# Routing one sequence earlier, folds of the queries in row groups, first rows tile by tile, and the last sequence's end by halves, in a two-layer recurrent/attention kernel

## The reference, cut to what matters

```python
x = L0_attn_h                                  # (8, 512, 256)
xn = _layernorm(x)
s = two gated recurrences over the tokens      # "minGRU", W0 then W1, each 256 -> 768
g = silu(top-1 routed expert MLP of xn)        # 8 experts, 256 -> 1024 -> 256, token by token
x = x + s * g
xn = _layernorm(x)
s = RWKV-like recurrence of xn                 # 16 heads, state 16x16 per head,
                                               # o = silu(g) * _ln(ys); s = o @ oW.T
g = silu(latent attention of xn, then a top-2 routed MLP of 8 experts and a shared one)
return x + s * g
```

## Time and profile before

| | |
|---|---|
| median of 3 runs | 2155.03 us (2154.07 to 2158.08) |
| the profiled execution: its own time | 2154.19 us |
| its span in the profile | 2152.3 us, 37412 instructions |
| busy: PE, DVE, ACT, POOL | 94%, 82%, 45%, 39% |
| phase A, B, C begin at | 0, 241.2, 541.2 us |

### The profile page before, as it was taken

One profiled execution on the slowest core, in us unless ns is written; L12 is line 12 of the kernel. 1 busy time (PEld: TensorE's weight loads), 2 busy tenths in 40 slices (PEclk: granted clock), 3 DMA queues, 4 the chain that ended last, 5 costly groups with the idle time before them and its releaser, 6 DMA issues.

```text
span 2152.3 us, 37412 instructions
## 1 busy us (share of the span) xinstructions
PE 2021.3 (94%) x11786; PEld 1235.5 (57%) x11787; DVE 1754.9 (82%) x2890; ACT 979.1 (45%) x2532; POOL 835.9 (39%) x666
## 2 busy tenths in 40 slices
PE   7998599999799999999999999999999999999996
PEld 4554399999446545644564465456445645654563
DVE  5998466665389888889888989898898888899886
ACT  3544244443248236623833472275238235722841
POOL 1335300000353345347434633553463446336431
PEclk9999799999799999999999999999999999999998
DMA  6544511121422212112221121122022212211320
GB/s 184 153 137 139 177 58 53 56 54 49 123 60 63 61 50 60 51 48 55 80 74 39 50 65 54 49 65 78 25 65 66 69 40 60 55 54 50 75 55 10
DMA packets 145729, 151.20 MB, mean 70 GB/s; under 512 B 47665, under 2 KB 105649, under 8 KB 145585
## 3 DMA queue, kind: packets, MB, share of 16 engines
q1 hardware_dynamic: 138288, 136.73, 23.4%
q0 software_dynamic: 3072, 8.41, 1.2%
q10 hardware_dynamic: 4224, 4.19, 0.7%
HBM read 121.71 MB, written 27.43 MB: 69 GB/s over the span
## 4 chain that ended last, share of the span: by engine, by line
PE 44%; issue 12%; DVE 10%; POOL 6%; ACT 3%; DMA 0%; POOLq 0%; DVEq 0%; ACTq 0%
PE bank L1382 14%; PE bank L1241 7%; PE bank L1258 5%; PE bank L1295 4%; PE bank L1395 3%; PE bank L1268 2%; POOL arena L2129 2%; PE bank L1244 2%; ACT arena L1623 2%; PE bank L1174 2%; POOL arena L2141 1%; PE bank L1452 1%; DVE arena L1866 1%; PE bank L1280 1%; DVE arena L1795 1%
## 5 line engine op out<-in xcount | busy, mean ns | idle before, releaser
L2121 POOL TENSOR_TENSOR arena<-arena 128x512 f32<-128x512 f32 x256 | 332.0, 1303 | 553.7 <-DVE arena L1842 539.9
L1382 PE MATMUL bank<-arena 128*128 128x256 f32 (+1 forms) x1120 | 374.1, 486 | 3.4 <-DVE arena L1987 3.4
L1842 DVE TENSOR_TENSOR_SCAN arena<-arena 128x512 f32<-128x512 f32 x256 | 363.6, 1420 | 1.1
L1174 PE MATMUL bank<-arena 128*128 128x512 f32 (+2 forms) x768 | 347.9, 601 | 1.0 <-ACT arena L1562 1.0
L1623 ACT ACTIVATE arena<-bank,arena 128x128 f32<-128x128 f32 (+3 forms) x512 | 266.7, 532 | 172.7 <-DVE arena L1822 172.4
L1382 PEld LDWEIGHTS bank<-arena 128*128 128x128 f32 x1120 | 207.3, 189 | 158.8 <-issue 127.8
L1822 DVE TENSOR_REDUCE arena<-bank 128x2 f32<-128x256 f32 (+3 forms) x256 | 207.9, 815 | 51.1 <-PE bank L1244 50.5
L1174 PEld LDWEIGHTS bank<-arena 128*128 128x128 f32 (+2 forms) x768 | 138.2, 186 | 188.4 <-issue 167.8
L1241 PE MATMUL bank<-arena 64*128 64x128 f32 (+3 forms) x1024 | 214.1, 495 | 28.4 <-ACT arena L1623 25.9
L1835 DVE TENSOR_TENSOR arena<-arena 128x512 f32<-128x512 f32 x256 | 225.3, 882 | 11.3 <-DMA arena<-values 9.7
L1632 ACT ACTIVATE arena<-bank 128x128 f32<-128x128 f32 (+3 forms) x512 | 197.9, 440 | 39.3 <-PE bank L1258 37.5
(11 more groups left out here) (207 smaller groups left out, 3039.3 us busy)
## 6 DMA issues: line engine op xcount, KB each, us to landing
arena<-values SPq DMA_DIRECT2D x256, 256.0 KB, 3.5
arena<-in_L_attn_h SPq DMA_DIRECT2D x16, 512.0 KB, 10.7
arena<-in_W1T SPq DMA_DIRECT2D x8, 1024.0 KB, 5.0
arena<-in_W2T SPq DMA_DIRECT2D x8, 1024.0 KB, 9.0
sorted_rows<-arena SPq DMA_DIRECT2D x42, 128.5 KB, 10.2
arena<-sorted_rows SPq DMA_DIRECT2D x40, 128.5 KB, 2.1
arena<-in_b2row SPq DMA_DIRECT2D x40, 128.0 KB, 2.9
gate_rows<-arena SPq DMA_DIRECT2D x39, 128.0 KB, 1.7
```

What stands on the lines that cost most here:

```text
L1174: last = nc.tensor.matmul(dst[rows, :], w, x, start=(n == 0), stop=(n == len(pairs) - 1))
L1382: last = nc.tensor.matmul(dst[o], w, x, start=first, stop=last_one)
L1842: nc.vector.tensor_tensor_scan(state[n % STATES][:, 1:T + 1], proj["w"][:, m, :], kv[n % 2], VEC["init"][:, m * HD + j:m * HD + j + 1], AL ...
L2121: nc.gpsimd.tensor_tensor(prods[(n + 2) % PRODS], state[n % STATES][:, 0:T], proj["r"][:, m, :], ALU.mult).then_inc(prod_done, 1)
```

## The change

Three parts.

In phase A, `ROUTED` becomes 6. Sequences 2 and 3 are both brought in early: the table `AHEAD_OF` says which sequences are normed, turned and scored in which step, a third buffer `h0` holds one more, and sequence 2 is normed at the end of step 0 and turned and scored inside step 1. At step 8 PE does unit (7, 2) ahead of `turn_out(6)`. SP issues the zero writes ahead of the expert's weights; three loads of weights (the second matrix of expert 6 and both of 7) are issued when the routing's small buffers are free.

At the start of phase C, all 64 records of `fold_queries` are issued ahead of `turn_head`, with the four row groups innermost, each to a bank of its own, and ACT's copies of them stand ahead of its norm. The first sequence's gathered rows are waited for one tile at a time (four semaphores in place of one, in every sequence), and `first_head` multiplies, adds and takes statistics by tile.

At the end, `read_out` goes ahead of the last two additions; centre, square (now ACT's), variance, root, reciprocal, scale and gate go by halves of the tokens; five banks take the place of one; the product, the residual and the store go by halves too.

```diff
@@ phase_a
-        ROUTED = B - 1
+        ROUTED = B - 2
+        AHEAD_OF = {0: (1,), 1: (2, 3), 2: (4,), 3: (5,), 4: (6,), 5: (7,)}
...
                 sp.wait_ge(gru_mm, UNIT_AT[b, 0] + 1)
-                expert_weights(b)
                 for z in range(6):
                     sp.dma_start(dram["sorted"][(6 * b + z) * P:(6 * b + z + 1) * P, :], zeros).then_inc(zeroed, 16)
+                expand_weights(b)
+                if b < B - 2:
+                    back_weights(b)
...
-            expert_weights(B - 1)
+            back_weights(B - 2)
+            expand_weights(B - 1)
+            back_weights(B - 1)
@@ phase_a, tensor
+                if s == 1:
+                    pe.wait_ge(scores_read, 2)
+                    turn_in(2)
                 if s == ROUTED:
                     ranks()
                     unit(s - 1, 2)
                     pe.wait_ge(route_read, 1)
+                    turn_out(s - 2)
+                elif s == B:
+                    unit(s - 1, 2)
                     turn_out(s - 2)
                 else:
@@ phase_c, tensor
-            def fold_queries(pair):
-                for i in (2 * pair, 2 * pair + 1):
-                    rows = slice(ND * i, ND * i + ND)
-                    for g in range(GROUPS):
-                        for k in range(KD):
-                            at = (g * KD + k) * ND
+            def fold_queries():
+                for g in range(GROUPS):
+                    for k in range(KD):
+                        at = (g * KD + k) * ND
+                        for i in range(HGROUP):
+                            rows = slice(ND * i, ND * i + ND)
                             last = nc.tensor.matmul(fold_bank[2 + i][:, at:at + ND], qn_w[rows, g, k * P:(k + 1) * P], kvb_w[rows, g, :],
                                                     start=True, stop=True)
...
-            fold_queries(0)
+            fold_queries()
             pe.wait_ge(xn_done, 1)
             for k in range(KD):
                 turn_head(k).then_inc(xn_turned, 1)
-            fold_queries(1)
@@ phase_c, vector
+            def first_head():
+                v.wait_ge(x_loaded, 32)
+                for i in range(NT):
+                    v.wait_ge(g_loaded[i], 16)
+                    nc.vector.tensor_tensor(s_in[:, i, :], s_in[:, i, :], g_in[:, i, :], ALU.mult).then_inc(x2_step, 1)
+                    v.wait_ge(x2_step, 3 * i + 1)
+                    nc.vector.tensor_tensor(s_in[:, i, :], x_in[:, i, :], s_in[:, i, :], ALU.add).then_inc(x2_step, 1)
+                    v.wait_ge(x2_step, 3 * i + 2)
+                    nc.vector.bn_stats(stats[:, i, :], s_in[:, i, :]).then_inc(x2_step, 1)
...
@@ phase_c, the end: tensor
-            mean_last(B - 1)
-            var_last(B - 1)
-            gates(B - 1, 0)
-            gates(B - 1, 1)
+            nc.tensor.matmul(bank[END_BANKS[0]][:, :], mean_m, y[:, 1, :], start=True, stop=True).then_inc(last_mm, 1)
+            for half in range(2):
+                pe.wait_ge(sq_done, 2 * B - 1 + half + 1)
+                nc.tensor.matmul(bank[END_BANKS[1 + half]][:, 0:2 * P], mean_m, sq[1][:, 2 * P * half:2 * P * (half + 1)],
+                                 start=True, stop=True).then_inc(last_mm, 1)
+            for half in range(2):
+                pe.wait_ge(o_done, 2 * B - 1 + half + 1)
...
@@ the end: scalar
+                    nc.scalar.activation(root, eps_d, ACT.Sqrt)
+                    for half in range(2):
+                        at = slice(2 * P * half, 2 * P * (half + 1))
+                        act.wait_ge(last_read, 4 * b + 1 + half + 1)
+                        nc.scalar.activation(sq[1][:, at], y[:, 1, at], ACT.Square).then_inc(sq_done, 1)
+                    for half in range(2):
+                        act.wait_ge(last_mm, 4 * b + half + 2)
+                        nc.scalar.activation(inv[1][:, 2 * P * half:2 * P * (half + 1)], bank[END_BANKS[1 + half]][:, 0:2 * P], ACT.Sqrt,
+                                             bias=eps_d[:, 0:1]).then_inc(last_read, 1)
                     silu_rows(b)
-                    root_last(b)
@@ the end: vector
+            end_parts(0)
+            end_parts(1)
+            end_rows_of(0)
+            end_rows_of(1)
```

More of the change, by code:

```diff
@@ L165, in phase_a @@
         top = mem.take(TILES)
-        scratch = Arena(spare.tensor, spare.at)
-        h0 = [spare.take(KD, T) for _ in range(2)]
+        last = spare.at + KD * F + 2 * FC * D
+        h0 = [spare.take(KD, T) for _ in range(HEADS)]
         gru_w = [spare.take(KD, 3 * D), mem.take(KD, 3 * D)]
-        cand, onehot, incl, excl = (scratch.take(TILES, E) for _ in range(4))
+        cand, onehot, incl, excl = (spare.take(TILES, E) for _ in range(4))
         slot_ge = spare.take(SLOTS, E)
@@ L175, in phase_a @@
         slot_e = spare.take(SLOTS)
+        assert spare.at <= last
         const_in = sem("const_in")
@@ L265, in score @@
                     for k in range(KD):
-                        last = nc.tensor.matmul(bank[6][:, i * E:(i + 1) * E], h0[b % 2][:, k, i * P:(i + 1) * P], cent[:, k, :],
+                        last = nc.tensor.matmul(bank[6][:, i * E:(i + 1) * E], h0[b % HEADS][:, k, i * P:(i + 1) * P], cent[:, k, :],
                                                 start=(k == 0), stop=(k == KD - 1))
@@ L558, in _ @@
             for s in range(ROUTED):
[L559 removed]
+                norm(AHEAD_OF[s][-1])
                 unit(s, 0)
@@ L565, in _ @@
                     unit(s - 1, 3)
+                else:
+                    norm(2)
             unit(ROUTED, 0)
@@ L1520, in _ @@
             experts(B - 1, True)
-            mean_last(B - 1)
-            var_last(B - 1)
-            gates(B - 1, 0)
-            gates(B - 1, 1)
+            pe.wait_ge(y_read, 2 * B)
+            nc.tensor.matmul(bank[END_BANKS[0]][:, :], mean_m, y[:, 1, :], start=True, stop=True).then_inc(last_mm, 1)
[5 more added lines that the diff above has]
+                pe.wait_ge(o_done, 2 * B - 1 + half + 1)
+                for i in (2 * half, 2 * half + 1):
+                    for c in range(KD):
+                        last = nc.tensor.matmul(bank[END_BANKS[3 + half]][:, (i % 2) * D:(i % 2 + 1) * D], y[:, c, i * P:(i + 1) * P],
+                                                o_w[:, c, :], start=(c == 0), stop=(c == KD - 1))
+                last.then_inc(last_mm, 1)
         @block.scalar
@@ L1555, in _ @@
                 nc.scalar.activation(q_by_head[:, k, :, ND:64], q_by_head[:, k, :, ND:64], ACT.Copy, scale=0.125).then_inc(q_folded, 1)
-            def fold_queries(pair):
-                act.wait_ge(q_mm, pair + 1)
-                for i in (2 * pair, 2 * pair + 1):
-                    for k in range(KD):
-                        src = fold_bank[2 + i][:, 0:GROUPS * KD * ND].rearrange("p (g k c) -> p g k c", g=GROUPS, k=KD)
-                        last = nc.scalar.activation(q_by_head[:, k, i:NH:HGROUP, 0:ND], src[:, :, k, :], ACT.Copy, scale=0.125)
-                last.then_inc(q_folded, 1)
+            act.wait_ge(q_mm, 1)
+            for i in range(HGROUP):
+                for k in range(KD):
+                    src = fold_bank[2 + i][:, 0:GROUPS * KD * ND].rearrange("p (g k c) -> p g k c", g=GROUPS, k=KD)
+                    last = nc.scalar.activation(q_by_head[:, k, i:NH:HGROUP, 0:ND], src[:, :, k, :], ACT.Copy, scale=0.125)
+            last.then_inc(q_folded, 1)
             norm_head(0)
@@ L2047, in between @@
                         ln_gate(b, 0)
-                    if e == ME:
+                    if e == ME and not final:
                         read_out(b, 1)
@@ L2196, in _ @@
             experts(B - 1, True)
-            square_last(B - 1)
-            g.wait_ge(g_loaded, 64 * B)
+            for i in range(NT):
+                g.wait_ge(g_loaded[i], 16 * B)
 IN_NAMES = ["L0_attn_h", "L0_attn_W0", "L0_attn_W1", "centT", "W1T", "W2T", "const",
```

131 lines of the change are left out of this document (85 added, 46 removed).

## The result

The changed kernel takes 2134.45 us (median of five runs, 2130.68 to 2137.28), the kernel before 2155.03. The ratio is 0.9903, interval 0.9889 to 0.9917; that is 20.9 us less, known to about 3 (20.6 by the two medians). The profiled execution took 2134.73, with a span of 2132.9.

A forecast was written before the change was run, and what follows sets the result against it. PE was 94% busy, so gains had to come from stretches where PE waits. 8.5 + 3.2 + 8.6 = 20.3 us off the profiled 2154.19 gave 2133.9, plus 0.84 for the runs' median: 2134.7, range 2130.5 to 2143.

The forecast's parts named there:

- Term A: End of phase A: earlier routing and scatter and reordered (7, 2) start phase B at 232.7, not 241.2; 8.5 us gained.
- Term C: End of phase C: earlier `read_out`, work by halves and a faster second product; 8.6 us gained, bounds 7.4 to 10.
- slower by the clock: Phase A, steps 6 to 8: PE waits for DVE and drops to the low clock; 2182 us, chance 0.03.
- Each unit of the DVE-paced stretch 0.6 longer: Phase A: nine units slowed, as a scatter beside them may do; phase B at 238, time 2140 us, chance 0.12.
- Most is the reordered (7, 2): Phase A: most of the 8.5 us comes from this order; without the earlier scatter only nothing to 0.3.
- Term B: Start of phase C: folds side by side and head by tiles start `before_attention` earlier; 3.2 us gained, bounds 0.9 to 5.0.
- The tiles: Start of phase C: first head done tile by tile ends at 554.3, against 555.08; 0.8 us gained.
- The rival with folds that don't overlap: Start of phase C: queries' folds run one by one, a loss of 4.8 us there; time 2142.7, chance 0.07.
- that rival: End of phase C: table reloads on the path or halves' hand-overs cut the gain to 5.5 us; 2138, chance 0.10.

The follow-up runs named there:

- the profile with the whole head: Changed kernel, but the first sequence's head waits for all four gathered tiles and works over all of them at once; one execution, 2129.74 us.
- the order alone: Kernel before, with only unit (7, 2) put ahead of `turn_out(6)` at step 8; 2155.46 us, ratio 0.9997.
- the routing alone: Changed kernel with step 8's order taken back, `turn_out(6)` ahead of (7, 2) again; 2141.39 us, ratio 0.9924.

## Why the prediction was right, step by step

Predicted 2134.7, measured 2134.45. The mechanisms were right in all three places, and the sum is closer than its terms: A was 2.8 too large for this profile, C 1.5 too small, and phase B, which nobody touched, gave 0.4 of its own (it takes 299.7 to 301.4 us in the profiles). Single runs of the changed kernel lie 6.6 us apart, so that the agreement to 0.3 is luck; by the profiles the terms are right to 1 to 3 us each.

**Term A, 8.5 predicted; 5.7 in the profile, 9.4 to 9.8 in three profiles where ACT was not late** (phase B at 231.4, 231.7 and 231.7; predicted 232.7), all against the one profile before; three other profiles with phase B's start set by the late scatter have it at 241.9 to 242.1. In the profile with the whole head the first scatter is at 171.62, forecast 171.6, which is luck: over all with the changed routing it is at 170.7 to 176.0, each time released by the zero writes. In that profile DVE starts its last unit at 220.8, forecast 219.1; 1.5 of that is the clock behind the wait of 2.03, the rival "slower by the clock" at one place out of nine. The sum has no term for the clock in step 1, where it costs 1.7 to 4.6. In the other direction I had put 3.1 between the store's landing and phase B. That was the distance from the scatter's landing; behind the store's it is 0.5, so this term was 2.6 too large. What the changed kernel's profile has beyond that one's is step 1's clock (1.5 left of 3.2) and ACT's late start (2.3). "Each unit of the DVE-paced stretch 0.6 longer" didn't happen: the first five units end 4.8 apart, as taken. "Most is the reordered (7, 2)" holds: it is worth some 4.5 by the times (6.8 in the traces, ACT's late start set aside), and nothing without the earlier scatter.

**Term B, 3.2 predicted, 3.1 measured at the first blend.** The path is the predicted one: line 1208 starts at 559.62, just behind DVE's last copy of the folded values at 559.5. Its parts differ. Folds 3.63, I had 3.1. By the Trainium skill ("TensorE: Matmul & The Clock Gate", Part 3), with its factor of 3.07 over one by one, I had given 4.0 as an estimate. The trace agrees: against the 11.38 measured here for the same 64 in sequence the factor is 3.1. It changes nothing, as I had said: ACT is done with the copies at 549.9 and has its norm at 550.8. The tiles brought 0.1 to 0.5 in single pairs instead of 0.8, which only the mean over all profiles shows. What made up for them in this profile is the first stretch of `before_attention`: 12 records in 7.37, before 7.95 (7.0 to 8.1 in the others with the changed start). The rival with folds that don't overlap, 2142.7, was close to the mark for what it would have cost: the run with the folds in sequence is at 2143.33.

**Term C, 8.6 predicted, 10.1 measured; 8.3 against the two profiles whose old end had the high clock in its second product.** The mean comes 1.25 earlier (forecast 1.2, shown by the run with the late `read_out`). The product starts 6.95 behind the first operation; forecast 6.7. The two products take 5.32, not 6.7: the clock rose earlier within them than I had taken (0.85 in 2126 to 2128). The last store and the end are 2.6, not 3.25: with half of the rows stored already, 0.8 is saved, not 0.2. ACT's table load (1.28 us at 2121.35) falls between root and Silu, beside DVE's reciprocal, so that rival fell.

## What to carry to other kernels

A reorder that measures as nothing isn't worthless while something else ends last: take the later of two ends away first, then time the reorder again (nothing and some 4.5 us for the same lines here). Matmuls with few rows should be issued with the row groups innermost, each to its own bank; 64 of them took 3.63 rather than 11.38 us. Before gains of a few us are hunted, look at the granted clock behind PE's waits: behind one of 2 us the low clock cost 1.7 to 4.6 us. Matmuls put into it kept the clock in two profiles of three, and the time they take must be set against that; count their records before choosing how many. And read a term of 1 or 2 us from more than one profile of each kernel: here the clock, ACT's late start and the gathers each move single profiles by as much.

## What the runs showed of the hardware that was not expected

The same program, with the same waits of 2 us on PE, has its clock fall differently from one execution to the next. In step 1 it fell in all eleven profiles without added work, for a shorter or longer time: `turn_in(2)` of the changed phase A starts between 40.9 and 44.1. At 190 it fell in three of nine and cost 1.7. The stretch from the first blend to `read_out`, the same code in all, took from 1544.7 to 1551.7 us in the profiles read here. Together these are of the size of the 6.6 us between single runs.

PE's work reached ACT and DVE late, measured by the end of PE's records, in five of nine profiles: `turn_out(6)` in four (ACT waited 3.9 to 4.6 us for it, DVE 2.3 to 3.1), (7,3) in one (2.3). The one profile each of the order alone and of the routing alone don't have it; with five of nine that may be chance. Less DMA traffic didn't cure it. No run here settles what does.
